# A routed layer before its experts: the list counts of a batch move into the next step, the lists are zeroed while they are filled, and the first rows are fetched before the stage ends

## What is computed

```
x = x + attention0(layernorm(x), ctx, ctx, mask)          # 16 heads
h = layernorm(x)
scores = h @ Wr.T + br ; w = softmax(scores)
idx = top2(scores + biases) ; val = w[idx] / sum(w[idx])
y = sum over the two chosen experts e of val_e * (silu(a_e) * b_e) @ Wl2_e
x = x + y
```

## Time and profile before

| | |
|---|---|
| median of three runs | 998.56 us (996.36, 998.56, 1004.04) |
| the profiled execution | 994.61 us, its span 992.7 us |
| first attention with its end | 0 to about 226 us of the span |
| expert stage begins on TensorE | 228.55 us |
| TensorE busy, whole span | 891.3 us (90%) |
| VectorE, ScalarE, GpSimd busy, whole span | 612.0, 469.1 and 379.8 us |
| moved by DMA | 137.78 MB, mean 139 GB/s |

### The profile page before, as it was taken

One profiled execution on the slowest core, in us unless ns is written; L12 is line 12 of the kernel. 1 busy time (PEld: TensorE's weight loads), 2 busy tenths in 40 slices (PEclk: granted clock), 3 DMA queues, 4 the chain that ended last, 5 costly groups with the idle time before them and its releaser, 6 DMA issues. The chain is left out here.

```text
span 992.7 us, 26217 instructions
## 1 busy us (share of the span) xinstructions
PE 891.3 (90%) x8784; PEld 758.1 (76%) x8785; DVE 612.0 (62%) x1561; ACT 469.1 (47%) x1209; POOL 379.8 (38%) x555
## 2 busy tenths in 40 slices
PE   4888889777999999997999899999999999779995
PEld 3677667636999999995556598888888887667784
DVE  3588788754455555542017466768667686549895
ACT  3777777712222222221333444445444454349895
POOL 4477677530000000006101446445464444426762
PEclk9998999987999999998999999999999999879998
DMA  4454447432433333315765798897989986411121
GB/s 119 145 164 145 143 148 237 140 145 94 128 108 93 98 93 108 93 44 181 262 225 180 165 188 185 179 182 164 200 172 176 172 178 150 90 33 55 60 61 49
DMA packets 222059, 137.78 MB, mean 139 GB/s; under 512 B 160289, under 2 KB 207393, under 8 KB 221857
## 3 DMA queue, kind: packets, MB, share of 16 engines
q1 hardware_dynamic: 180304, 99.78, 40.1%
q10 hardware_dynamic: 38608, 28.64, 10.8%
q0 software_dynamic: 3072, 8.39, 2.6%
HBM read 81.79 MB, written 54.98 MB: 138 GB/s over the span
## 5 line engine op out<-in xcount | busy, mean ns | idle before, releaser
L1717 ACT ACTIVATE c_pT<-c_T 128x512 f32<-128x512 f32 (+2 forms) x90 | 50.2, 595 | 104.4 <-PE c_T L1876 73.3
L1666 POOL TENSOR_TENSOR c_soft<-c_soft,c_share 128x616 f32<-128x616 f32 (+2 forms) x96 | 70.3, 760 | 63.4 <-DVE c_share L2129 61.8
L1062 ACT ACTIVATE b_rowsT<-b_RT 128x256 f32<-128x256 f32 x39 | 15.0, 383 | 158.2 <-PE b_RT L1104 158.2
L1173 DVE COPY b_w<-moe_w 128x1024 f32 x78 | 53.5, 687 | 56.2 <-issue 50.7
L1676 POOL MEMSET d_round<- 128x1 f32 x1 | 0.1, 98 | 226.5 <-POOLq L953 226.5
L1113 PEld LDWEIGHTS b_G<-b_rowsT,b_w 128*128 128x128 f32 x624 | 77.2, 195 | 4.2 <-DVE b_w L1173 1.5
L1113 PE MATMUL b_G<-b_rowsT,b_w 128*128 128x128 f32 x624 | 77.9, 279 | 1.5 <-ACT b_rowsT L1062 1.3
L1113 PE MATMUL b_U<-b_rowsT,b_w 128*128 128x128 f32 x624 | 76.1, 275 | 0.0
L1187 DVE SCALAR_TENSOR_TENSOR b_hidT<-b_U,b_bias,b_gate 128x128 f32<-128x128 f32 x156 | 43.9, 343 | 51.9 <-PE b_U L1113 45.4
L1140 PE MATMUL b_Y<-moe_w,b_hidT 128*128 x312 | 73.9, 380 | 0.9 <-DVE b_out L1218 0.9
L1113 PEld LDWEIGHTS b_U<-b_rowsT,b_w 128*128 128x128 f32 x624 | 72.9, 192 | 0.0
(11 more groups left out here) (231 smaller groups left out, 2167.2 us busy)
## 6 DMA issues: line engine op xcount, KB each, us to landing
rel_windows<-c_relw ACTq DMA_DIRECT2D x28, 368.0 KB, 6.7
c_bias<-rel_windows SPq DMA_DIRECT2D x16, 616.0 KB, 5.6
prob_rows<-c_soft SPq DMA_DIRECT2D x16, 616.0 KB, 7.3
moe_w<-in_L_Wl SPq DMA_DIRECT2D x16, 512.0 KB, 4.1
early<-in_L_early SPq DMA_DIRECT2D x16, 384.0 KB, 3.2
values<-c_pT ACTq DMA_DIRECT2D x22, 256.0 KB, 3.8
b_rows<-expert_lists SPq DMA_DIRECT2D x39, 128.0 KB, 2.0
expert_out<-b_out SPq DMA_DIRECT2D x39, 128.0 KB, 1.7
```

The source lines that it names most:

```text
L1173: nc.vector.tensor_copy(own[p][h][:, :, :], w1[:, bass.ds(e, 1), :, h * HE:(h + 1) * HE].rearrange("p o c n -> p (o c) n"))\
L1666: ins = nc.gpsimd.tensor_tensor(soft[p][:, hs, a:z], soft[p][:, hs, a:z], share[:, s, hs].unsqueeze(2).to_broadcast([P, HS, z - a]), ALU.mult)
L1717: nc.scalar.activation(dst, view(T[k]), ACT.Copy, **kw).then_inc(g["emptied"], 1)
```

## The change

- **List counts.** `places`, the four list operations and `scatter` are for batch b-4 and stand in the front part of step b: `places` on TensorE behind the first probabilities, the list operations on VectorE between `attention_out` and `maxima(b, 0)`, `scatter` on GpSimd ahead of everything else. There is one more step, b = 19, for the last batch.
- **Zeros.** `pad` is gone, with its conversion of the counts to integers. Instead SyncE writes zeros over rows b*128 to b*128+127 of all eight lists in each step b below 16, one DMA of 1 MB, and `scatter(b)` waits for it.
- **End of the stage.** All text copies are ScalarE's. SyncE waits for the tile numbers and all scatters and issues the loads of the first two row tiles before the engines meet; VectorE reads the first two experts' numbers there too. The wait for the text copies' landing moves into the expert stage, on VectorE ahead of the second expert's weights.

```
@@ sync
+            def fill(b, i, p):
+                since(sp, s_fill[p], 16 * i)
+                block_rows = t["lists"].rearrange("(e r) d -> r e d", e=NE)[bass.ds(b * P, P)]
+                sp.dma_start(block_rows, zeros[:, :].unsqueeze(1).to_broadcast([P, NE, D])).then_inc(s_fill[p], 16)
             def steps(b, i, p):
                 if there(b + 2):
                     load_context(b + 2, p)
+                if there(b):
+                    fill(b, i, p)
                 if there(b + 4):
                     load(b + 4, p)
...
             by_batch(steps)(sp)
-            pad(sp, 0)
-            for n in range(EARLY_HALVES - 4, EARLY_HALVES - 2):
-                text_store(sp, n, text_dv, n - 3)
-            padded(sp, 0)
-            for out in shared["s_text_out"][:2]:
-                sp.wait_ge(out, 16 * EARLY_HALVES // TEXT_BANKS)
+            sp.wait_ge(s_tiles, 1)
+            for p in range(2):
+                sp.wait_ge(s_sc[p], 32 * (NB // 2))
+            for n in range(2):
+                shared["load_rows"](sp, n, n)
@@ gpsimd
-            def scatter(b, p):
+            def scatter(b, i, p):
+                apart(pool, s_fill[p], 16 * (i + 1))
                 apart(pool, g["slot"], b + 1)
...
             def steps(b, i, p):
+                if there(b - 4):
+                    if there(b - 2):
+                        apart(pool, g["p_sb"], 4 * (b - 2) + HPT)
+                    scatter(b - 4, i - 2, p)
                 if there(b + 3):
                     std(0, b + 3)
...
-                if there(b - 3):
-                    if there(b - 1):
-                        apart(pool, g["p_sb"], 4 * (b - 1) + HPT)
-                    scatter(b - 3, 1 - p)
@@ scalar
-            pad(act, 1)
-            text_values(range(EARLY_HALVES - 2, EARLY_HALVES))
-            padded(act, 1)
+            text_values(range(EARLY_HALVES - 4, EARLY_HALVES))
@@ tensor
                     probabilities(b - 1, 1 - p, 0)
+                if there(b - 4):
+                    places(b - 4)
                 if there(b):
                     scores(b, p)
...
-                if there(b - 3):
-                    places(b - 3)
@@ vector
                 if behind:
                     attention_out(den)
+                if listed:
+                    row = list_rows(b - 4, list_counts(b - 4))
+                    list_slots(b - 4, i - 2, p, list_sums(b - 4, row))
                 if there(b):
                     maxima(b, 0)
...
-                if lists:
-                    row = list_rows(b - 3, list_counts(b - 3))
-                    list_slots(b - 3, i - 2 + p, 1 - p, list_sums(b - 3, row))
...
+            shared["first_experts"] = [shared["expert_of"](dve, n) for n in range(2)]
@@ vector, expert stage
-            e_out = expert_of(dve, 0)
-            e_ahead = expert_of(dve, 1)
+            e_out, e_ahead = shared["first_experts"]
             for p, e in enumerate((e_out, e_ahead)):
+                if p == 1:
+                    for out_copy in shared["s_text_out"]:
+                        dve.wait_ge(out_copy, 16 * EARLY_HALVES // TEXT_BANKS)
                 gate_weights(p, p, e)
```

More of the change, by code:

```diff
@@ L302, in text_halves @@
         def text_halves(b):
-            return {NB: range(0, 1), NB + 1: range(1, 3), NB + 2: range(3, 4)}[b]
+            return {NB: range(0, 1), NB + 1: range(1, 3), NB + 2: range(3, 4), NB + 3: range(0)}[b]
         block = ctx.enter_context(nc.Block())
[L307 to L315, removed]
         def text_part(n):
@@ L868, in steps @@
             def steps(b, i, p):
-                front, ahead, behind, lists = there(b + 3), there(b + 1), there(b - 2), there(b - 3)
+                front, ahead, behind, lists, listed = there(b + 3), there(b + 1), there(b - 2), there(b - 3), there(b - 4)
                 if behind:
@@ L967, in experts @@
         tile_expert, tile_row = shared["tile_expert"], shared["tile_row"]
-        rows = [sb(f"b_rows{p}", [P, D]) for p in range(2)]
+        rows = shared["rows"]
         rowsT = [sb(f"b_rowsT{p}", [P, KD, P]) for p in range(2)]
@@ L989, in experts @@
         s_clear = sem("b_clear")
-        s_in = [sem(f"b_in{p}") for p in range(2)]
+        s_in = shared["s_rows"]
         s_out = [sem(f"b_out_{p}") for p in range(2)]
@@ L1018, in _ @@
         def _(sp):
-            def load(n, p):
-                at = tile_row[0:1, n:n + 1] if isinstance(n, int) else tile_row[0:1, bass.ds(n, 1)]
-                row = sp.value_load(at, min_val=0, max_val=NE * ROWS_E - P)
-                since(sp, g["rt_mm"], n - 1)
-                sp.dma_start(rows[p][:, :], t["lists"][bass.ds(row, P)]).then_inc(s_in[p], 16)
             def store(n, p):
@@ L1029, in steps @@
             def steps(n, i, p):
-                load(n, p)
+                if not isinstance(n, int) or n > 1:
+                    shared["load_rows"](sp, n, p, g["rt_mm"])
                 if there(n - 3):
@@ L2598, in load_experts, with expert_of, load_rows @@
                               one(t["L0_Wl2"])[:, half * HE // 2:(half + 1) * HE // 2].rearrange("e (k p) n -> p (e k) n", p=P)).then_inc(s, 16)
+            shared["rows"] = [moe.enter_context(nc.sbuf_tensor(f"moe_rows{p}", [P, D], F32)) for p in range(2)]
+            shared["s_rows"] = [ctx.enter_context(nc.semaphore(f"s_rows{p}")) for p in range(2)]
+            def expert_of(eng, n):
+                at = shared["tile_expert"][0:1, n:n + 1] if isinstance(n, int) else shared["tile_expert"][0:1, bass.ds(n, 1)]
+                return eng.value_load(at, min_val=0, max_val=NE - 1)
+            shared["expert_of"] = expert_of
+            def load_rows(sp, n, p, read=None):
+                at = shared["tile_row"][0:1, n:n + 1] if isinstance(n, int) else shared["tile_row"][0:1, bass.ds(n, 1)]
+                row = sp.value_load(at, min_val=0, max_val=NE * ROWS_E - P)
+                if read is not None:
+                    since(sp, read, n - 1)
+                sp.dma_start(shared["rows"][p][:, :], t["lists"][bass.ds(row, P)]).then_inc(shared["s_rows"][p], 16)
+            shared["load_rows"] = load_rows
             shared["experts_ready"] = 16 * 4 * NE
```

32 lines of the change are left out of this document (10 added, 22 removed).

## The result

| | before | after |
|---|---|---|
| median, 10 runs each | 996.04 us (993.74 to 1004.04) | 1005.62 us (1003.05 to 1008.42) |
| profiled execution | 994.61 us, its span 992.7 us | 1004.2 us, its span 1002.4 us |
| first to last step of the mask loop, M of step 4 to M of step 12 | 93.2 us, 11.65 a step | 104.66 us, 13.08 a step |
| last a_S product ends | 221.07 us | 235.58 us |
| first b_RT product | 228.55 us | 238.97 us |

The ratio is 1.0088, with a 95% interval of 1.0065 to 1.0111: the changed kernel is slower by 0.9%, 9.6 us by the medians and 9.7 by the two spans. The forecast was 12 us slower. Ratios leave out slow executions, of which there is one in all, 1752.45 us among the eight of e4.

What follows compares the result with a forecast made beforehand. A loop over the mask's load, 11.23 us a step, was taken to bound the first attention. Steps through 12 +15.0, behind the loop +1.4, end -4.4 give +12.0 us on 998.56: 1010.6 us, range 994 to 1022.

Steps and rivals of the forecast that it cites:

- The loop over the mask: Steps 4 to 12: maxima, `out_var`, `std`, `masks`, load, `norm_stats`, `attention_out`, maxima; 11.23 us alone, steps growing to 13.1.
- M12: Start of VectorE's first maxima (M) in step 12, where the eight intervals forecast at 104.8 us end.
- Rival 1: Steps 4 to 12: total work of VectorE, ScalarE and GpSimd sets the step; 995.5 us, no change; chance 0.18.
- M4: Start of VectorE's first maxima (M) in step 4; 1.3 us added for the list in that step.
- the 3.4 us that weren't its own: Part of the 93.2 us from step 4 to 12 outside the loop; growth 11.6 if all covered, 15.0 if none.
- Rival 2: TensorE's 18.7 us wait for `chosen` ahead of `places` was the bound; 989.5 us, faster; chance 0.08.
- Rival 3: SyncE's fills of zeros don't go through between bursts, masks come 1 to 2 us later; 1024 us; chance 0.15.
- Behind the loop: After step 12: +0.6 us for GpSimd's part, +1.4 for later slots lengthening `std(1)`'s wait in steps 16 and 17.
- The end: End of the stage: row loads issued before the engines meet, so TensorE starts on the experts 4.4 us earlier, or 2.4.
- The sum: Whole kernel: 15.0 + 1.4 - 4.4 = +12.0 us, about 1% slower; chance 0.55.
- The other costs taken as nothing: `places` on TensorE: 0, to 0.5 us a step; fills: 0, to 2 a step; scatter's landing: 0, to 2 once.
- the two terms of the loop: Per step: +1.3 us for the list behind the mask's landing on VectorE, +0.55 for the scatter ahead of `std` on GpSimd.

Runs made afterwards that it cites:

- e4: Changed kernel with the list operations moved ahead of `norm_stats` and its mask wait on VectorE; ratio 0.993 to the kernel before.
- e2: Kernel before with list work, `places` and scatter moved as in the change, no fills, old end; ratio 1.0132 to the kernel before.
- e8: Changed kernel with the scatter moved between `std(1)` and `masks` on GpSimd; ratio 1.0358 to the kernel before.
- e9: Kernel before with the load divided, rows and mask each with a semaphore; ratio 0.9995 to the kernel before.
- e3: Changed kernel with list work, `places` and scatter put back, fills and new end kept; ratio 0.9952 to the kernel before.
- e11: e3 with the load divided into rows and mask; ratio 0.9949 to the kernel before.
- e1: Kernel before with only `places` moved on TensorE, behind the first probabilities of the next step; ratio 0.9988 to the kernel before.
- e12: Changed kernel with a second 1 MB DMA of zeros behind each fill, to an unread tensor; ratio 1.0171 to the kernel before.
- e7: e4 with the load divided, rows asked for at the step's head, mask alone behind `keep`; ratio 0.9897 to the kernel before.
- e5: Changed kernel with `masks(b+2)` first in GpSimd's step, ahead of the scatter; ratio 0.9987 to the kernel before.
- e6: e5 with the list operations also ahead of `norm_stats`, as in e4; ratio 0.9972 to the kernel before.

## Why the prediction was right, point by point

**The loop over the mask.** Forecast: steps of 13.1 us, M12 14.4 us later. Measured: 13.08 on average, M12 at 165.96 instead of 152.20, 13.8 later. That this is the cause is shown by e4, which takes it away by moving the list ahead of the wait, by e2, which has it alone, and by e8, which makes it longer. Rival 1 (the work sets the step) fails for the changed kernel by e4: the same work takes 1.74 us a step less. For the kernel before it is nearly right: with the mask's loop open the step shrinks by no more than 0.5 us (e9; 0.6 from e3 to e11). The prediction overstated how much of a bound the mask was there. It did no harm, since the loop was only made longer.

**How the terms split.** Growth from M4 to M12 was 11.4 us against a forecast of 13.1. The text had 11.6 as the case in which the longer loop covers all of the 3.4 us that weren't its own, and took the middle, 13.1. The measured growth looks like that case, but only in part for its reason. Of the 3.4 us, 1.9 were covered, 1.4 of which e1 takes away with TensorE's wait. The other 1.5 were the one mask that landed after 4.5 us. A longer loop doesn't cover such a load; it just didn't come again, and the slowest mask of the changed kernel's loop took 3.5 us. That is luck: with one as late as before, the growth would have been some 12.9. On the other side M4 is 2.3 us later instead of 1.3. Of that, 1.2 were there at M of step 3 already (49.17 against 48.01), where no list exists; e3 has 0.7 of it and e2, without fills, 2.9. So it varies among kernels, and no run isolates it.

**Rival 2** (TensorE's wait is the bound) is refuted by e1: all of the wait removed, and no gain clear of noise. "It is ScalarE's copy that comes next" held, with 17.0 us of it.

**Rival 3** (the fills don't go through) is refuted for one fill a step by e3, whose steps are those of before. It was closer than the prediction made it sound. A fill lands 8.8 us behind its issue in the median. Counted as the prediction counts, from the mask's issue to the landing of the fill, it is 11.6 to 13.6 us in the eight steps, inside its 10.6 to 13.7, but at the slow end. In the step shown the fill goes out at 139.23 and lands at 147.6, 0.6 us ahead of the next mask's issue. Two windows in front of that issue at 148.26, with share and GB/s in the last two columns:

```profile
144.00:145.00 1.00, 1.00 (x26) 0.78 (x29) 0.57 (x2) 1.00 (x6) 0.77 (x3) 0.86 1.10 395
...
147.00:148.00 1.00, 0.78 (x8) 0.54 (x5) 0.58 (x4) 0.56 (x3) 0.72 (x3) 1.00 0.03 10
```

It isn't always so: of the 12 fills that have a mask behind them, four land 0.3 to 1.5 us after that mask's issue, and the mask takes 2.9 to 3.6 us. The margin is thin, and e12 is past it.

The prediction cites the Trainium skill ("DMA: Bandwidth & Descriptors", Queues, rings and completion order) for descriptors of one queue being consumed in ring order. e12 agrees: none of the 11 masks issued behind unfinished zeros landed ahead of them, and the four with the most zeros left took 3.9 to 6.3 us.

**Behind the loop.** Forecast +0.6 and +1.4. This is the step of the sum that missed, though the mechanism didn't. Up to the last `rows_normal` (223.62 after, 207.38 before) the growth is 16.2 us, 2.5 more than at M12, against 2.0 forecast. `rows_normal` waits for a scatter's landing three times there, 0.98, 2.37 and 1.38 us, up to 204.43. But from there to the last slots it is 5.7 us instead of 7.4, and these 1.7 us the prediction hadn't seen. In the kernel before one half of the text product stands ahead of the last `places`, and it ran slow. TensorE in a window before (columns: busy time by engine, granted clock, DMA share, GB/s), and TensorE's own rows there:

```profile
210.00:213.60 3.60, 3.60 (x7) 1.72 (x8) 1.15 (x8) 0.30 (x1) 1.02 (x2) 0.53 0.20 73
```

```profile
210.23 3.53 PE L664 MATMUL a_S<-a_text_w,a_text_c 128*128 128x512 f32 x4
213.59 0.28 PE L652 MATMUL a_T<-early,const 128*128 128x8 f32 x2
```

And after:

```profile
226.00:228.40 2.40, 2.40 (x12) 1.43 (x12) 1.15 (x8) 0.40 (x2) 1.88 (x2) 1.00 0.32 117
```

```profile
226.31 1.96 PE L656 MATMUL a_S<-a_text_w,a_text_c 128*128 128x512 f32 x4
228.11 0.28 PE L644 MATMUL a_T<-early,const 128*128 128x8 f32 x2
```

The same four products take 3.53 us at a granted clock of 0.53 (1.2 GHz nearly throughout) and 1.96 at 1.00 (2.4 GHz). In the 3 us ahead of each, TensorE was busy for 2.10 us in both kernels, at a clock of 0.50 before and of 1.00 after. What decides between the two isn't in these rows. But the fast half isn't of the list's making: e1 and e3, with the list where it was, have 1.96 us too. Of the fourteen traces only before and e9 have a slow half here. In the twelve others the slow stretch falls one step earlier, where two halves take 5.2 to 6.7 us instead of 3.68 (in the changed kernel 5.92 at 0.62), and costs less: in the changed kernel VectorE waits 0.54 us for the `places` behind them. So nearly all of the 1.7 us (3.53 less 1.96) lies in where the slow stretch fell, and the change can't be credited with it.

**The end.** Forecast -4.4 us, measured -4.1 (3.39 instead of 7.49 us of idle time on TensorE), confirmed by e3, which has the same 3.39 and is 4.8 us faster than before by its ratio. The last event before the meeting was ScalarE's last text store, as forecast: issued at 236.25, 0.34 long,

```profile
236.25 0.34 ACTq L313 DMA_DIRECT2D values<-a_text_v  x1
```

and from its end to TensorE's first product it is 2.4 us, where I had 1.7. Of the wait for the text copies that the change moves, GpSimd's 6.44 us in front of L1037 is what the profile shows, and nobody waits for it: TensorE and VectorE start in the same microsecond.

**The sum.** Growth of the loop 11.4 (forecast 13.1), ahead of it 2.3 (1.3), behind it 0.8 up to the last slots (2.0), the end -4.1 (-4.4), and -0.7 over the rest of the span, which no one row explains: 9.7 us by the spans, against 12.0. No term was wrong by more than 1.7 us, and the errors went both ways. Two of the differences, the late mask and the slow text half, are events of the one trace of before rather than work of the change.

**The other costs taken as nothing.** `next_rows` did get the wait for L832 that was named, 17.7 us in 10 times. e2 has it too (15.3 us), and e4, which hasn't, differs by no more than the two terms of the loop; so it seems to have stayed in TensorE's slack. The scatter's landing was waited for in the three places named above, 4.7 us in all, where the forecast had 0 to 2 us once.

## What to carry to other kernels

Work that stands ahead of a wait for a load is cover: before it is moved behind the wait, follow the load back to what lets it be issued, for if that is set going by what now stands behind the moved work, the move is paid in full in every step (with everything else the same, this kernel is 0.9% slower than before with the list work behind the wait, and 0.7% faster with it ahead). The largest wait in a table needn't be the one to remove; take it away in a run by itself, as e1 does, and see which wait takes its place. A median time to landing hides the few loads that set the long steps; look at each load beside what was issued ahead of it in its queue, as in e12. A load that brings two things for two readers can be divided, so that each part waits only for its own buffer; the fastest kernel here (e7, 0.9897) has it, but no pair of runs shows its gain by itself beyond their intervals.

## What was unexpected of the hardware

- GpSimd's first indirect DMA started 4.8 to 5.8 us behind its slots in the four kernels with the divided load, and 1.0 us behind them in the others, except where masks or standard deviations stood between (e5, e6, e8). In these four and in e8, where 2.80 us of idle time have no releaser, it started 2.0 us behind a packet of the DMA kind "instruction" that moved in the gap. A few more instructions ahead on an engine can, it seems, put a load of instructions on the path.
- A fill of 1 MB took 8.8 us to its landing in the median, and a second one behind it in the same queue 11.1 us. A 64 KB load issued behind them landed in 3.1 and 3.2 us in the median, but never ahead of them, and after 3.9 to 6.3 us where they had over 3 us left.
- TensorE's granted clock was at half, 1.2 GHz, through 3 us in which it was busy for 2.10 and for most of a 3.5 us stretch of unbroken products, and a text half took 3.53 us instead of 1.96. By their durations, every one of the fourteen traces has such a slow half in one of the last two steps with text; in two of them it lay right ahead of the last list.
